# First cross attention of a two-layer block: sums of squares on column quarters of TensorE, scores on 64 rows at a time

## What is computed

```
def _L0_xattn_ref(x, y, Wq, bq, Wk, bk, Wv, bv, ..., qn_w, qn_b, kn_w, kn_b, ...):
    ...
    q = _ln((x @ Wq + bq).reshape(b, s1, H, HD), qn_w, qn_b)
    kv = jnp.concatenate([y_main @ Wk + bk, y_main @ Wv + bv], axis=-1)
    kv = kv.reshape(b, s2, H, 2 * HD)
    k = _ln(kv[..., :HD], kn_w, kn_b)
    v = kv[..., HD:]
    qT = q.transpose(0, 2, 1, 3)
    ctx = _attn(qT, k.transpose(0, 2, 1, 3), v.transpose(0, 2, 1, 3))
    ...
x = x + _L0_xattn_ref(_layernorm(x, axis=-1), ctx_1024, ...)
```

## Time and profile before

| | us |
|---|---|
| median of 3 runs | 2640.07 (2638.02 to 2644.95) |
| the profiled execution | 2640.4 |
| its span | 2638.6 |
| main loop of the stage, first to last score matmul | 140.0 to 851.0 |

### The profile page before, as it was taken

One profiled execution on the slowest core, in us unless ns is written; L12 is line 12 of the kernel. 1 busy time (PEld: TensorE's weight loads), 2 busy tenths in 40 slices (PEclk: granted clock), 3 DMA queues, 4 the chain that ended last, 5 costly groups with the idle time before them and its releaser, 6 DMA issues. The chain is left out here.

```text
span 2638.6 us, 43489 instructions
## 1 busy us (share of the span) xinstructions
PE 2371.9 (90%) x15316; PEld 1912.3 (72%) x15316; DVE 1667.7 (63%) x2670; ACT 1167.3 (44%) x2108; POOL 1039.0 (39%) x724
## 2 busy tenths in 40 slices
PE   4599999999999599996997899999999998788866
PEld 2588887878887388884776688888888876566644
DVE  3458777777878333334542388878888883666663
ACT  1334444444444233332322376766676662332242
POOL 3158777867877300000110055554455550100230
PEclk8699999999999699997998999999999998899979
DMA  3000000000000112112322000000000001211200
GB/s 108 1 26 26 26 1 26 26 13 15 26 1 1 54 60 64 64 36 52 77 49 105 24 18 26 26 18 18 19 26 26 1 1 64 62 42 38 77 0 17
DMA packets 104268, 89.74 MB, mean 34 GB/s; under 512 B 32752, under 2 KB 82432, under 8 KB 104080
## 3 DMA queue, kind: packets, MB, share of 16 engines
q1 hardware_dynamic: 103792, 87.28, 10.9%
q0 software_dynamic: 288, 0.00, 0.0%
HBM read 86.22 MB, written 1.05 MB: 33 GB/s over the span
## 5 line engine op out<-in xcount | busy, mean ns | idle before, releaser
L2179 POOL TENSOR_TENSOR xT<-xT,x1b_ring 128x512 f32<-128x512 f32 (+1 forms) x176 | 249.2, 1416 | 213.3 <-ACT x1b_ring L2309 207.0
L864 POOL TENSOR_TENSOR x0b_krstd<-x0b_krstd,minus_half 128x24 f32<-128x24 f32 x64 | 267.0, 4172 | 128.8 <-DVE x0b_krstd L928 96.5
L884 POOL TENSOR_TENSOR xT<-xT,x0b_ring 128x512 f32<-128x512 f32 (+1 forms) x176 | 248.8, 1414 | 116.9 <-ACT x0b_ring L1073 105.7
L1073 ACT ACTIVATE x0b_ring<-x0b_ring 128x512 f32<-128x512 f32 (+1 forms) x208 | 131.0, 632 | 235.4 <-DVE x0b_ring L956 227.6
L820 PE MATMUL x_ps<-x0b_qbd,x0b_kT 128*128 128x256 f32 (+1 forms) x832 | 231.9, 402 | 0.0
L111 DVE TENSOR_TENSOR x1b_plo<-x1b_ring,x1b_phi 128x512 fp32r<-128x512 f32 (+1 forms) x208 | 221.5, 1065 | 6.8 <-issue 4.6
L978 DVE TENSOR_TENSOR x0b_ring<-x_ps,x0b_krstd 128x512 f32<-128x512 f32 (+1 forms) x208 | 143.0, 687 | 93.7 <-PE x_ps L820 83.1
L2324 ACT ACTIVATE x1b_ring<-x_ps,x1b_keymask 128x512 f32<-128x512 f32 (+1 forms) x208 | 143.1, 688 | 131.2 <-DVE xT L2251 125.9
L116 PE MATMUL x_ps<-x1b_qy,x1b_yT 128*128 128x512 f32 (+1 forms) x416 | 175.9, 423 | 4.3 <-ACT x1b_ring L2324 2.9
L988 DVE TENSOR_TENSOR xT<-xT,x0b_ring 128x512 f32<-128x512 f32 (+1 forms) x176 | 165.4, 940 | 6.0
L2251 DVE SCALAR_TENSOR_TENSOR xT<-x_ps,x1b_keymask,xT 128x512 f32<-128x512 f32 (+1 forms) x176 | 131.3, 746 | 58.4 <-PE x_ps L118 57.5
(11 more groups left out here) (580 smaller groups left out, 5810.3 us busy)
## 6 DMA issues: line engine op xcount, KB each, us to landing
x_y<-in_ctx_dram SPq DMA_DIRECT2D x8, 1536.0 KB
x_y<-in_ctx_dram SPq DMA_DIRECT2D x24, 512.0 KB, 4.0
a_wn<-in_L_attn_W_Q_dram SPq DMA_DIRECT2D x16, 256.0 KB, 3.1
a_wn<-in_L_attn_W_K_dram SPq DMA_DIRECT2D x16, 256.0 KB, 3.5
a_wn<-in_L_attn_W_V_dram SPq DMA_DIRECT2D x16, 256.0 KB, 4.1
a_won<-in_L_attn_W_O_dram SPq DMA_DIRECT2D x16, 256.0 KB, 2.9
x1a_wq<-in_L_xattn_Wq_dram SPq DMA_DIRECT2D x4, 1024.0 KB, 10.6
x1c_wo<-in_L_xattn_Wo_dram SPq DMA_DIRECT2D x8, 512.0 KB, 7.0
```

What stands on the lines that cost most here:

```text
L864: ins = g_.tensor_tensor(r, r, c.minus_half[:, 0:8].unsqueeze(1).broadcast_to([P, whole, 8]), ALU.pow)
L884: g_.tensor_tensor(total[half][0:m, :], old, src, ALU.add).then_inc(summed, 1)
L2179: g_.tensor_tensor(total[half][0:m, :], old, src, ALU.add).then_inc(summed, 1)
```

## The change

Three things change, all in `x0_main_attention`.

1. **Sums of squares.** W now has the small operand `heads32` (128 by 32, eight columns in use) as weights and 128 columns of `sq` streaming; key tile t of the chunk writes partitions 32t to 32t + 31, so 12 or 16 MATMUL rows on three or four column quarters. The result has keys on columns. ScalarE copies it to SBUF (`wsb`), and a new operation T, one step or more later, turns it back with one transpose; VectorE and GpSimd take T where they took W.
2. **Scores.** Each matmul of 128 rows by 256 columns becomes two of 64 rows (two heads) by 128 columns: rows 64 to 127 (r = 1) of tile n alternate with rows 0 to 63 (r = 0) of tile n + 1. So there are 8 MATMUL rows per tile, the first half of a tile is scored one step ahead, and its waits (`begin_scores`) come one step ahead too. Three score banks; the wait in step n is again that tile n - 2 has been taken.
3. **Banks.** The third score bank is paid for by `X_BANK`: flips and spreads of maxima, sums and inverse sums now rotate through the three banks of K, W, V, Y and T, 59 uses in 26 steps. VectorE applies the inverse sums at step 30 of a half in place of 31.

```
-        HERE = entries("0:K030 1:K031 2:W03 3:K100 4:K101 5:W10 5:V0 6:K110 6:V1 7:K111 7:V2 8:W11 9:K120 9:V3 10:K121 10:V4 "
-                       "11:W12 12:V5 12:V6 13:K130 14:K131 15:W13 16:V7 18:V8 19:V9 20:Va 21:Vb 22:Vc")
+        HERE = entries("0:T02 0:K030 1:K031 2:W03 3:T03 3:K100 4:K101 5:W10 5:V0 6:T10 6:K110 6:V1 7:K111 7:V2 8:W11 9:T11 "
+                       "9:K120 9:V3 10:K121 10:V4 11:W12 12:T12 12:V5 12:V6 13:K130 14:K131 15:W13 16:T13 16:V7 18:V8 19:V9 "
+                       "20:Va 21:Vb 22:Vc")
+        AHEAD = entries("11:Y00 13:Y01 16:K000 17:K001 17:Y10 17:Y11 18:W00 19:T00 19:K010 20:K011 21:W01 22:T01 22:Y20 "
+                        "22:Y21 23:K020 23:Y30 24:K021 24:Y31 25:W02")
...
-        S_BANK, O_BANK, M_BANK, X_BANK, KV_BANKS = 0, 2, 4, 7, (3, 5, 6)
+        S_BANKS, O_BANK, M_BANK, KV_BANKS = (0, 1, 2), 3, 4, (5, 6, 7)
...
                         pe.wait_ge(sq_done, 16 * seq + (8 * half + 2 * j + 2))
-                        for t in range(n):
-                            m = size(t0 + t)
-                            for g in range(2):
-                                mm = pe.matmul(out[0:m, 8 * t + 4 * g:8 * t + 4 * g + 4], sq[g][:, t * P:t * P + m],
-                                               headsum[:, :], start=True, stop=True)
+                        for g in range(2):
+                            for t in range(n):
+                                mm = pe.matmul(out[32 * t:32 * t + 32, 0:P], heads32[:, g, :], sq[g][:, t * P:(t + 1) * P],
+                                               start=(g == 0), stop=(g == 1), skip_group_check=True)
...
+                    if kind == "T":
+                        _, half, j = e
+                        rows = 32 * chunks[j][1]
+                        pe.wait_ge(w_kept, 8 * seq + (4 * half + j + 1))
+                        pe.transpose(out[:, 0:rows], wsb[0:rows, :], c.ident[0:rows, 0:rows]).then_inc(w_turned, 1)
...
+                def begin_scores(seq, n):
+                    half, kt = n // KT, n % KT
+                    if kt == 0:
+                        pe.wait_ge(q_placed, 8 * seq + (4 * half + 4))
+                    if kt in (0, 3, 6, 9):
+                        pe.wait_ge(k_done, 16 * seq + (8 * half + 2 * (kt // 3) + 2))
+                    if TILES * seq + n >= len(S_BANKS):
+                        pe.wait_ge(kept, TILES * seq + n - len(S_BANKS) + 1)
+
+                def scores(seq, n, g, r):
+                    half, kt, i = n // KT, n % KT, 2 * g + r
+                    rows = slice(64 * r, 64 * r + 64)
+                    return pe.matmul(ps[:, S_BANKS[(TILES * seq + n) % len(S_BANKS)], i * P:(i + 1) * P],
+                                     kT[rows, g, kt * P:(kt + 1) * P], qbd[rows, 2 * half + g, r * P:(r + 1) * P],
+                                     start=True, stop=True)
...
+                        after = part != "last" or n < TILES - 1
+                        if after:
+                            begin_scores(*((seq, n + 1) if n < TILES - 1 else (seq + 1, 0)))
+                        pe.wait_ge(begun, TILES * seq + n + 1)
                         for g in range(2):
-                            mm = pe.matmul(ps[0:m, S_BANK + n % 2, g * GC:(g + 1) * GC], kT[:, g, kt * P:kt * P + m],
-                                           qbd[:, 2 * half + g, :], start=True, stop=True)
-                        mm.then_inc(scored, 1)
+                            mm = scores(seq, n, g, 1)
+                            if g == 1:
+                                mm.then_inc(scored, 1)
+                            if after:
+                                mm = scores(*((seq, n + 1) if n < TILES - 1 else (seq + 1, 0)), g, 0)
+                        if after:
+                            mm.then_inc(begun, 1)
...
+                    if e[0] == "W":
+                        _, half, j = e
+                        rows = 32 * chunks[j][1]
+                        act.wait_ge(w_made, 8 * seq + (4 * half + j + 2))
+                        if (seq, half, j) != (0, 0, 0):
+                            act.wait_ge(w_turned, 8 * seq + (4 * half + j))
+                        act.activation(wsb[0:rows, :], src[0:rows, 0:P], ACT.Copy).then_inc(w_kept, 1)
```

More of the change, by code:

```diff
@@ L683, in x0_main_attention, with put @@
         place, uses = {}, [0] * 8
-        for seq in range(-1, B):
-            part = "before" if seq < 0 else "last" if seq == B - 1 else "body"
-            for ahead, e in [x for n in range(TILES) for x in ([(1, e) for e in AHEAD.get(n, [])] if seq < 0 else
-                                                               made_at(part, n))]:
-                bank = KV_BANKS[sum(uses) % len(KV_BANKS)]
-                place[seq + ahead, e] = bank, uses[bank]
-                uses[bank] += 1
+        def put(name):
+            bank = KV_BANKS[sum(uses) % len(KV_BANKS)]
+            place[name] = bank, uses[bank]
+            uses[bank] += 1
+        for e in BEFORE:
+            put((0, e))
+        for seq in range(B):
+            part = "first" if seq == 0 else "last" if seq == B - 1 else "body"
+            for n in range(TILES + 18 if part == "last" else TILES):
+                for what, at in (("sums", 29), ("inverse", 30), ("maxima", 13)):
+                    f = half_at(part, n, at)
+                    if f is not None:
+                        put((what, 2 * seq + f))
+                for ahead, e in made_at(part, n):
+                    put((seq + ahead, e))
         kv_full, kv_free = [st.sem(f"kv_full{i}") for i in range(8)], [st.sem(f"kv_free{i}") for i in range(8)]
@@ L795, in step @@
                     if f is not None:
+                        bank, nth = place["sums", 2 * seq + f]
+                        pe.wait_ge(kv_free[bank], nth + 1)
                         pe.wait_ge(summed, (KT - 1) * (2 * seq + f + 1))
[L798 removed]
                         for t in range(4):
[L800 removed]
+                            mm = pe.transpose(ps[:, bank, t * P:(t + 1) * P], total[f % 2][:, t * P:(t + 1) * P], c.ident[:, :])
```

91 lines of the change are left out of this document (54 added, 37 removed).

## The result

Over four runs of each, the changed kernel takes 2604.9 us (median) against 2641.6: ratio 0.986, interval 0.984 to 0.988. It is faster by 37 us, where 75 were forecast. The profiled execution of after has a span of 2599.4 us against 2638.6, 39.2 less.

The account below looks back on a forecast made before the run. TensorE's own stream was taken to bind. Middle sequences: 92.1 - 10.4 - 7.5 + 1.0 + 5.1 + 1.8 = 82.1 us; with first and last, 2640.4 - 75 = 2565 us, range 2542 to 2605.

Parts of the forecast that it names:

- What bounds the kernel: Main loop: TensorE's own stream binds; next come VectorE at 74.5 us and GpSimd at 71.9 per sequence.
- Scores, sums of squares, changes of form: TensorE per sequence: scores -10.4 us, sums of squares -7.5, 30 more switches between full matmuls and tiles +5.1.
- Waits that come: Main loop: new waits of TensorE for other engines and banks, +1.8 us per sequence, bounds 0 and 4.
- (a): Steps 5 and 25: W waits for the squares of the K before it, about 0.6 us per sequence.
- (b): Shared banks come back sooner while VectorE has its heaviest stretch, steps 3 to 7: 1.2 us per sequence.
- (c): Maxima, inverse and sums no longer wait for each other on bank 7: nothing gained.
- First and last sequence: Loop's ends: first sequence -8.4 us with more switches of matmul form; last -7, limited by VectorE.
- The end behind the last score: GpSimd's and VectorE's work after the last score stays as it was.
- lockstep: Eight hand-overs per sequence where TensorE needs VectorE's last result become exposed, 0.5 us each: +32 us, about 2597; chance 0.20.
- the test named for it: TensorE's waits for L111's kin, L1037 or the bank-freeing lines sum to over 30 us in the loop.
- Scores gain nothing: Score matmuls: weights can't load while the same 64 rows stream; blocks stay 0.87 us, total 2630 to 2643; chance 0.06.
- The clock rival: Main loop: sparser TensorE work lowers the mean clock; at 0.85 the time is 2667 us; chance 0.06.

Follow-up runs that it names:

- x_light: f_pow with VectorE's running maximum taken on 64 of its 512 columns, the rest left out; 2577.0 us, ratio 0.976.
- w_only: The kernel before with only the sums of squares on column quarters and the turning back T; 2620.8 us, ratio 0.993.
- f_pow: The changed kernel with GpSimd's power of T02 after its sum of step 1 and not before it; 2592.4 us, ratio 0.981.
- s_only: The changed kernel with the sums of squares as before and no T; 2677.6 us, ratio 1.014.
- s_wide: s_only with each weight load of W streaming 64 columns and not 4, as many instructions; 2640.3 us, ratio 0.999.
- x_best: f_pow with queries placed at steps 9 and 21, not 6 and 19, and Y31 made ahead of K021 in step 24; 2576.4 us, ratio 0.976.
- f_all: f_pow with queries placed a step earlier, T10 behind K110 and V1, and Y11 a step later; 2588.6 us, ratio 0.981.
- x_best3: x_best with queries placed at the end of steps 8 and 21, and Y11 moved from step 17 to 18; 2591.8 us, ratio 0.984.
- x_noalt: The changed kernel with both upper score halves issued, then both lower ones, not taking turns; 2612.9 us, ratio 0.990.
- w_pow: w_only with GpSimd's power of T02 moved behind its sum of step 1; 2608.8 us, ratio 0.989.

## Why the prediction was wrong, point by point

- **What bounds the kernel**: right as far as it went. TensorE's stream bound the loop before, and shortening it shortened the time. That VectorE with 74.5 us and GpSimd with 71.9 would come next was the wrong picture: x_light took 64 us off VectorE and gained 10. The sign named for it failed as well: VectorE's wait for scores was to fall from 83 to 20 or 40 us, and is 74.8.
- **Scores, sums of squares, changes of form**: right. 80.3 - 92.1 = -11.8 us per sequence was forecast, and busy time fell by 90.13 - 78.36 = 11.8. Added up from start to start over these two sequences, score blocks went from 22.0 to 17.2 us, W from 11.2 to 3.6, T came with 0.6, and all else together grew by 0.1. So W (-7.6) and the scores with all changes of form (-4.7, where -10.4 + 5.1 = -5.3 was forecast) came out well, T cheaper than forecast (0.6 and not 1.0), and that the sum fits to the tenth is luck. The 0.17 us for a change were not measured by themselves; in a score block the first pair of rows stands 0.21 from the second and the last 0.21 from what follows, where 0.11 is the pace.
- **Waits that come**: the step that failed. +1.8 us per sequence was forecast with bounds 0 to 4; at full clock idle time rose by 6.9. Over the six middle sequences it rose by 38.7 us where 10.8 were forecast, and these 28 us are the bulk of the 36 that are missing. Another 4 to 5 there are busy time: it fell by 66, not 71, as more of after's sequences have stretches at the lower clock. Line by line, per sequence: (a) squares 0.6 was forecast, 9.6 / 8 = 1.2 came (2.0 / 8 before). (b) named the right stretch, steps 3 to 7, and even the sum behind a power of 4.2 us, and gave 1.2 us for all of it; the sums alone wait up to 2.0 (13.7 / 8 = 1.7 on average) and K111 another 0.9 to 1.2. The working took the length of a power from the earlier trace rows but never set its start against the moment at which the sums are turned. It also gave no price to what happens when VectorE's placing of queries meets GpSimd's additions, and the placing doubled. (c) gave nothing for turning maxima and inverse in the shared banks, since bank 7 had never been waited for. But its having been free was the point: Y11 now waits 1.1 us for the inverse's bank. The maxima in step 0 cost 1.2 and were in no term; w_only has 0.7 of them, so they come in part with T.
- **First and last sequence**: -3.3 and -3.8 against -8.4 and -7. By the same term in part: TensorE's idle time rose by 3.8 us in the first, where 1 was forecast, and by 6.0 in the last. The first also ran at a clock of 0.94 where the forecast used a row at 0.98.
- **The end behind the last score**: it was to stay, and took 43.4 us against 41.0 (43.2 in f_pow). GpSimd has 18 operations behind the last score where it had 17, and the mean clock there is 0.53 and not 0.58; no run tells which of these it was.
- **Rivals**: lockstep had the right size, 2597, and the test named for it came true, if barely: after's waits for squares, for L111 and for banks sum to 9.6 + 4.2 + 18.0 = 31.8 us. Its mechanism, eight hand-overs of maxima, sums and inverse at 0.5 us each, is only part of it: sums and maxima flipped wait 22.1 us in the whole loop, two of the eight and not all, and the larger of the two is a wait for GpSimd and not for VectorE. "Scores gain nothing" fell: 0.64 us and not 0.87. The Trainium skill's rule in TensorE: Matmul & The Clock Gate, Part 3, The mechanism, that weights load beside a running matmul only when the row group differs, goes with the 0.87 of this rival; here the measurement decides against it, as pairs of rows with weights of their own start 0.11 us apart, half of the 0.22 that the rows of 256 columns took before: the streaming alone, with no time for the weights on top. The clock rival didn't decide the time of after: the loop's mean clock is 0.98 against 0.99. Yet its mechanism is real: s_only's loop is 40 us longer than s_wide's by the clock for the most part, and after has 12 us more busy time in its loop than f_pow.
- **The range**, 2542 to 2605, took in 2604.9 by its last tenth of a microsecond, thanks to the lockstep case alone; that is luck. The forecast's own 2542 to 2590 did not.

**What stays open.** Of TensorE's 38.7 us of idle time in x_best, 11.3 are waits of W for squares and 13.9 for banks that VectorE frees late. Whether one order of the table removes them isn't known: two tries (f_all, x_best3) moved them. Why a hole of 2 us brings the clock down in one sequence and not in the next isn't known either, nor what brings it down in the kernel before. The loop of each kernel was profiled once, so the part of a difference in loops that is clock rests on single executions.

## What to carry to other kernels

Once a stream has 10% of slack taken out, compare moments, not loads: for every point where the engine needs another's last result, set the start of the longest instruction in that other queue against it, as the next bound is often one queued instruction and not an engine's sum. When a change makes one hand-over later (T here), look at what then stands behind the later work in the next engine's queue, and reorder it: here the power went behind the addition. And when a bank that nobody waited for is given to other work, count who takes it next and what frees it.

## What the runs showed of the hardware

- Four fp32 matmuls on 64 rows and 128 columns, as eight rows of the profile, take 0.64 us with the change of form, whether the halves alternate (after) or come in pairs (x_noalt, 0.65). The rows start in pairs, 0.11 us apart.
- Blocks with four columns per weight load beside scores on half of the rows run the loop at a mean clock of 0.92 (s_only). With 64 columns, and all else alike, it is 0.98, and the loop 40 us shorter (s_wide). TensorE shows as busy for all of the row at 0.50 in s_only's windows, so a full TensorE column doesn't tell this apart.
- A stop of 2.0 us was followed at once by a stretch at 0.53 in every second middle sequence of after; without the stop the loop's mean clock was 1.00 (f_pow, and w_pow against w_only's 0.99). The kernel before has such stretches too, without a stop.
- L964, 32 partitions from SBUF to SBUF on VectorE, takes 0.27 to 0.34 us. If it begins while a GpSimd addition (512 columns) runs, it ends 0.08 us behind the addition, up to 1.3 us after its own start (after). The four that ran within one power of GpSimd (24 columns, 4.2 us) in the kernel before took 1.28 us together. The Trainium skill has a cause in SBUF — State Buffer, SBUF: two separate sides: one pair of ports shared by the two engines, locked for a whole instruction by whichever begins first. The additions agree with it; the power doesn't, as nothing was held up beside it, and no run here shows the ports.
